# Four-layer graph network: layer 0's norm and first aggregate of the next batch placed in the tail of the present one

## The reference

```python
# layer 0: aggregate, two linear maps with an RMS norm and silu between
neighbor_sum = jnp.einsum('bnm,bmd->bnd', adjacency, x); agg = epsilon * x + neighbor_sum
h = silu(_rmsnorm(agg @ W1 + b1, rms_weight)); out = h @ W2 + b2          # 256 -> 1024 -> 256
# layer 1: one linear map, sigmoid(s1_i + s2_j) * adj, rows divided by their sums
# layer 2: masked attention, 8 heads of 32, edge bias W_e[h] * adj, softmax over 512
# layer 3: D^-1/2 adj D^-1/2 (x @ weight) + bias
```

## Time and profile before

| | before |
|---|---|
| median of 3 runs (lowest to highest) | 3917.56 us (3916.5 to 3918.57) |
| the profiled execution, its own time | 3917.78 us |
| its span | 3916.0 us |
| PE busy | 3609.4 us, 92% of the span |
| DVE / ACT / POOL busy | 67% / 58% / 21% |
| mean granted TensorE clock | 0.994 |
| mean busy share of 16 DMA engines, q1 | 26.2% |

### The profile page before, as it was taken

How to read it: one execution, slowest core, us unless ns; L and a number is a source line. 1 busy time by engine, 2 the same in 40 slices (tenths; PEclk the granted TensorE clock), 3 DMA queues, 4 the chain that set the end, 5 groups by cost and what they waited for, 6 DMA issues and landing times.

```text
span 3916.0 us, 67010 instructions
## 1 busy us (share of the span) xinstructions
PE 3609.4 (92%) x19375; PEld 2448.1 (63%) x19596; DVE 2623.3 (67%) x6436; ACT 2273.2 (58%) x5029; POOL 824.0 (21%) x1611
## 2 busy tenths in 40 slices
PE   5899999999999999999999999999999999999997
PEld 3566666666666666666666666666666666666664
DVE  4566766667666666666667666676666676666674
ACT  2555665555665556655556655556655566655564
POOL 1122111222112222212221122221122221122210
PEclk9899999999999999999999999999999999999999
DMA  2222222322222322223222223222233222232212
GB/s 77 60 78 75 64 67 64 86 65 75 65 67 73 85 66 65 75 54 86 72 78 59 70 65 86 65 70 70 57 83 81 70 65 75 54 86 68 78 48 65
DMA packets 166929, 274.99 MB, mean 70 GB/s; under 512 B 23906, under 2 KB 59874, under 8 KB 166756
## 3 DMA queue, kind: packets, MB, share of 16 engines
q1 hardware_dynamic: 166756, 273.45, 26.2%
HBM read 122.37 MB, written 16.78 MB: 36 GB/s over the span
## 4 chain that ended last, share of the span: by engine, by line
PE 45%; issue 26%; DVE 14%; POOL 9%; ACT 5%; POOLq 1%; SPq 0%; DVEq 0%; DMA 0%; ACTq 0%; another core or an unknown queue 0%
PE turn L1186 9%; PE front L999 6%; PE front L1000 5%; PE score L1176 5%; PE front L1001 5%; POOL small L366 4%; PE score L1177 4%; PE value L1201 3%; PE front L1052 3%; DVE pT L788 2%; ACT hf L485 2%; PE front L1041 2%; DVE hid L780 2%; DVE small L840 2%; POOL x_out L430 2%
## 5 line engine op out<-in xcount | busy, mean ns | idle before, releaser
L574 ACT ACTIVATE prob<-prob,small 128x512 f32<-128x512 f32 x1024 | 736.2, 719 | 443.6 <-DVE small L863 442.0
L863 DVE CUSTOM_DVE_ANT_0 prob<-score,adj_sb,drv 128x512 f32<-128x512 f32 x1024 | 762.4, 747 | 252.0 <-PE score L1177 133.7
L1186 PE MATMUL turn<-ident,prob 128*128 128x128 f32 x4096 | 616.1, 275 | 14.8 <-ACT pT L583 8.9
L1186 PEld LDWEIGHTS turn<-ident,prob 128*128 128x128 f32 x4096 | 483.5, 141 | 135.5 <-issue 45.7
L583 ACT ACTIVATE pT<-turn 128x512 f32<-128x512 f32 x768 | 446.6, 584 | 143.4 <-PE turn L1186 143.4
L1176 PE MATMUL score<-qk_stack 128*128 128x512 f32 x1024 | 486.9, 479 | 20.7 <-DVE small L863 19.1
L999 PE MATMUL front<-w_hi,s_hi 128*128 128x256 f32 x1024 | 353.7, 345 | 28.1 <-DVE x_in L767 28.1
L655 DVE TENSOR_TENSOR s_lo<-front,s_hi 128x512 fp32r<-128x512 f32 x320 | 219.1, 685 | 154.1 <-ACT s_hi L471 152.3
L1177 PE MATMUL score<-unlinked,neg_mask 128*128 128x512 bf16 x803 | 313.8, 391 | 0.0
L388 POOL TENSOR_TENSOR small<-small 128x1 f32<-128x1 f32 x128 | 24.7, 193 | 1265.7 <-ACT aside L518 1265.7
L1000 PE MATMUL front<-w_lo,s_hi 128*128 128x256 f32 x1024 | 288.6, 282 | 0.0
(11 more groups left out here) (158 smaller groups left out, 7547.7 us busy)
## 6 DMA issues: line engine op xcount, KB each, us to landing
qk_stack<-qk SPq DMA_DIRECT2D x1024, 128.0 KB, 2.4
adjT_f<-in_adjT SPq DMA_DIRECT2D x32, 1024.0 KB, 5.2
adj_sb<-in_adj SPq DMA_DIRECT2D x32, 1024.0 KB, 7.9
prob<-in_adjT SPq DMA_DIRECT2D x32, 1024.0 KB, 5.3
x_in<-in_x SPq DMA_DIRECT2D x32, 512.0 KB, 3.5
out<-x_out SPq DMA_DIRECT2D x32, 512.0 KB, 2.9
pT<-in_W SPq DMA_DIRECT2D x2, 1024.0 KB
rmsw_b<-in_rmsw SPq DMA_DIRECT2D x1, 512.0 KB
```

The costliest lines, as they stand in the source:

```text
L574: act.activation(prob[:, i % 8, :], prob[:, i % 8, :], ACT.Exp, bias=nmax[:, h, n:n + 1], scale=-1.0, accum_out=prsum[:, h, n:n + 1]).then ...
L863: dve.tensor_tensor_reduce(out=prob[:, i % 8, :], in0=SB_[i % 2][:, :], in1=adj_sb[:, n, :], scale=neg_w[:, h:h + 1], scalar=3e38, op0=ALU ...
L1186: last = pe.transpose(TB[k % 2][:, tile(n)], prob[:, (4 * h + n) % 8, tile(j)], ident[:, :])
```

## The change

Batch nx = tf+1 enters a phase. Its layer-0 norm and aggregate are done in the tail of the phase (t, tf), instead of at the opening of the next one.

- PE: `aggregate` is cut in two. Its first half stands after `aggregate3(t, 1)`, then come `turn(tf)` (which had opened the next phase), `project3(t)`, and the second half. The next phase opens with the Q and K projections, then `hidden` of row tile 0, a half of the values, the other `hidden`, the other half. Those two `hidden` products and their squares are no longer in the grid.
- DVE: `stats0(nx)` ahead of layer 1's two low parts, `diagonal(nx)` ahead of `update1`, the low parts of the aggregate and the copy of `turn` around `update3`.
- ACT: the norm of nx between `attended1` and `gathered`; POOL: its scale ahead of `add_b3`, and `add_b2` at the end of the phase.
- SP: x of the following batch is loaded at the start of a phase, ahead of the stacks, into a buffer of its own.
- Buffers: `x_new` is added (x as loaded; `add_b2` writes x_in from it). The normed x of layer 0 (`h0`) lies in `hid`. `x_out` now lies over `qk`, so ACT's first write of `qk` in a phase waits for the store of the batch before. Layer 3's high and low parts lie over `vals` and `unlinked` and not in T_hi and T_lo; `inv_x` lies over `hb`.

```diff
+        x_new = sb("x_new", [P, NT, D])
+        h0 = hid[:, :].rearrange("p (n d) -> p n d", n=NT)
-        x_out = sb("x_out", [P, NT, D])
+        x_out = sb("x_out", [P, NT, D], over="qk")
+        a3_hi = sb("a3_hi", [P, DT, N], F32R, over="vals")
+        a3_lo = sb("a3_lo", [P, DT, N], F32R, over="unlinked")
...
+            def phases(t, tf, nx):          # SP
+                if nx is not None:
+                    sp.wait_ge(b2_added, at(tf, 1, 1))
+                    sp.wait_ge(f_norm["ready"], at(tf, 8, 4))
+                    load_x(nx)
                 if t is not None:
+                    for h in range(H):
+                        stack(t, h)
...
             def add_b2(tf):                 # POOL
-                pool.wait_ge(f_norm["ready"], at(tf, 8, 4))
+                pool.wait_ge(x_loaded, at(tf, 16, 16))
+                if later(tf):
+                    pool.wait_ge(x1_ready, at(tf, 4, 0))
...
                     layernorm(t, 1, b_norm, norm_tiles(50), dinv)
+                if nx is not None:
+                    layernorm(nx, 0, f_norm, norm_tiles(0))
+                if t is not None:
                     add_b3(t)
...
             def qk_high(t, g, i):           # ACT
                 act.wait_ge(qk_ps, at(t, 4, 2 * g + i + 1))
+                if g == 0 and i == 0 and later(t):
+                    act.wait_ge(out_stored, t * 16)
...
                     attended1(tf, 1)
+                if nx is not None:
+                    norm0(nx)
                 if b:
                     gathered(t, 0)
                     gathered(t, 1)
                 if f:
                     layernorm(tf, 0, b_norm, norm_tiles(50), x2, hf)
+                if nx is not None:
+                    aggregated(nx, 0)
+                if f:
+                    turned(tf)
+                if nx is not None:
+                    aggregated(nx, 1)
...
                     update2(t)              # DVE
                     means(t, 1, b_norm, norm_tiles(50))
+                if nx is not None:
+                    stats0(nx)
                 if f:
                     attended1(tf, 0)
                     attended1(tf, 1)
                     factors1(tf)
+                if nx is not None:
+                    diagonal(nx)
                 if f:
                     update1(tf)
                     means(tf, 0, b_norm, norm_tiles(50))
                 if b:
                     gathered(t, 0)
                     gathered(t, 1)
+                if nx is not None:
+                    aggregated(nx, 0)
+                if f:
+                    turned(tf)
+                if b:
                     update3(t)
+                if nx is not None:
+                    aggregated(nx, 1)
+                    restore_diagonal(nx)
...
                 if b:                       # PE
-                    turn(t)
                     project_qk(t, 0, 0)
                     project_qk(t, 0, 1)
+                if f:
+                    hidden(tf, 0, 0)
+                if b:
                     project_v(t, 0)
                 if f:
-                    aggregate(tf)
+                    hidden(tf, 0, 1)
                 if b:
                     project_v(t, 1)
...
                     aggregate3(t, 1)
+                if nx is not None:
+                    aggregate(nx, 0)
+                if f:
+                    turn(tf)
+                if b:
                     project3(t)
+                if nx is not None:
+                    aggregate(nx, 1)
```

More of the change, by code:

```diff
@@ L111, in gnn_kernel @@
         msg = region[:, 5120:6144].rearrange("p (n d) -> p n d", n=NT)
-        inv_x = sb("inv_x", [P, NT, HG, HD], over="x_out")
+        inv_x = sb("inv_x", [P, NT, HG, HD], over="hb")
         small = sb("small", [P, 236])
@@ L431, in add_b3, with phases @@
                 ins.then_inc(b3_added, 1)
[L433 to L436, removed]
+            def phases(t, tf, nx):
                 if t is not None:
@@ L457, in phases @@
                     layernorm(tf, 0, b_norm, norm_tiles(50))
-            phases(None, 0)
-            phases(0, 1)
-            with pool.Fori(1, B - 1) as t:
-                phases(t, t + 1)
-            phases(B - 1, None)
+                if nx is not None:
+                    add_b2(nx)
+            layernorm(0, 0, f_norm, norm_tiles(0))
+            add_b2(0)
+            phases(None, 0, 1)
+            phases(0, 1, 2)
+            with pool.Fori(1, B - 2) as t:
+                phases(t, t + 1, t + 2)
+            phases(B - 2, B - 1, None)
+            phases(B - 1, None, None)
         @block.scalar
@@ L912, in update3, with phases @@
                                              in1=x_out[:, n, :], op0=ALU.mult, op1=ALU.add).then_inc(out_ready, 1)
-            def opening(t, tf):
-                b, f = t is not None, tf is not None
-                if b:
-                    turned(t)
-                if f:
-                    stats0(tf)
-                    diagonal(tf)
-            def rest(t, tf):
+            def phases(t, tf, nx):
                 b, f = t is not None, tf is not None
@@ L1017, in _, with aggregate @@
             pe.wait_ge(setup_dve, SETUP_DVE)
-            def aggregate(tf):
-                pe.wait_ge(f_norm["ready"], at(tf, 8, 4))
-                pe.wait_ge(diag_eps, at(tf, 1, 1))
-                if later(tf):
-                    pe.wait_ge(x1_ready, at(tf, 4, 0))
-                for d in range(DT):
-                    for m in range(NT):
-                        last = pe.matmul(FB[d][:, :], hf[:, m, tile(d)], adjT_f[:, m, :], start=(m == 0), stop=(m == NT - 1))
-                    last.then_inc(agg_ps, 1)
+            def aggregate(tf, d):
+                if d == 0:
+                    pe.wait_ge(f_norm["ready"], at(tf, 8, 4))
+                    pe.wait_ge(diag_eps, at(tf, 1, 1))
+                    if later(tf):
+                        pe.wait_ge(msg_ready, at(tf, 4, 0))
+                for m in range(NT):
+                    last = pe.matmul(FB[d][:, :], h0[:, m, tile(d)], adjT_f[:, m, :], start=(m == 0), stop=(m == NT - 1))
+                last.then_inc(agg_ps, 1)
             def hidden(tf, n, c):
@@ L1232, in step @@
                 def step(n, k, start, stop):
-                    return product(proj3_bank(n), (T_hi[:, k, tile(n)], T_lo[:, k, tile(n)]),
+                    return product(proj3_bank(n), (a3_hi[:, k, tile(n)], a3_lo[:, k, tile(n)]),
                                    (w3_hi[:, k, :], w3_lo[:, k, :]), start, stop)
```

128 lines of the change are left out of this document (63 added, 65 removed).

## The result

| | before | changed |
|---|---|---|
| median (lowest to highest) | 3917.7 us (3916.5 to 3918.57) | 3794.1 us (3793.83 to 3796.3) |
| span of the profiled execution | 3916.0 us | 3792.0 us |
| PE busy | 3609.4 us, 92% | 3595.9 us, 95% |
| ratio, 95% interval | | 0.9686 (0.9669 to 0.9703) |

The change saves 123.6 us, 3.2%. 3813 was forecast, a saving of 104.8, so the direction and the range held and the size was 15% short.

The account below looks back on a forecast made before the run. PE's matmul stream was taken as the bound, with only its idle time to win: 3917.8 - 102 (30 full boundaries) - 5 (first boundary) + 2 (last) = 3812.8, so 3813 us, range 3790 to 3850.

Parts of the forecast that it names:

- PE's stream is the bound and its idle time at the boundary is the prize: Between phases: PE's matmuls bound the kernel; of some 7.2 us idle a period, 4.6 stand at the boundary.
- 3.4 us a boundary: Each of 30 boundaries between full phases: idle time falls from 4.62 to 1.2 us, 102 us in all.
- The 1.2 us that I left idle: Idle left at a boundary: 0.15 at the turn, 0.05 in project3, 1.0 over scores 2, 3 and 4.
- Which part gives what: At the boundary: aggregate's move removes waits of 0.88, 0.97 and 0.93 us; hidden's earlier place removes the silu's 1.29.
- The four tail queues take the work at no cost: Phase tail: DVE, ACT, POOL and SP fit the added work into gaps, the diagonal with 0.5 us to spare.
- First boundary, 5 us: After the front-half-only phase: half the aggregate fills 3.55 us, 0.97 goes, the grid's start gains about 0.8.
- Last boundary, 2 us lost: Last boundary, no batch to aggregate: the turn waits for hf, and ACT for the store; 2 us slower.
- The two covers: Full phases: x_out's store has 1.6 us of cover before Q's high part, 1.1 more until K's; stacks have 1.3.
- Rival C: Opening: store or stacks land late and stop it; decides at 6.9 us, gain gone at 10.3; chance 0.06.
- Rival B: Phase tail: POOL's add holds DVE, the update starts 1.5 us late, saving 1.9 a boundary, 3858 us; chance 0.13.
- Rival E: Boundary: score waits smaller than counted and other waits shrink too, saving 4.2 to 4.6 us, middle 3783; chance 0.07.

Follow-up runs that it names:

- run 1: The changed kernel with row tile 0's two hidden products and squares back in the grid, values directly after the Q and K projections: 3863.9 us, ratio 0.9867.
- Run 3: The changed kernel with three extra 128x512 copies on DVE between the diagonal and layer 1's update: 3829.2 us, ratio 0.9773.
- run 7: The kernel before with 7 extra 128x512 matmuls on constants in the first phase's tail, where PE idles: 3918.4 us, ratio 1.0000.
- run with 512 KB: The changed kernel with an extra 512 KB DMA (rows of x) issued by SP just ahead of the store of x_out: 3848.1 us, ratio 0.9824.
- run with 1 MB: The changed kernel with an extra 1 MB DMA (adjacency rows) issued by SP just ahead of the store of x_out: 3927.5 us, ratio 1.0023.

## Why the prediction was right, point by point

- *PE's stream is the bound and its idle time at the boundary is the prize*: right. 4.60 us of idle became 0.95, the rest of the period stayed.
- *3.4 us a boundary*: the mechanism was right, the term too small. A boundary saves 3.92. The 1.2 us that I left idle were 0.95, of them 0.90 in two score waits of 0.55 and 0.35, not three of 0.5, 0.1 and 0.4, and none in project3. The turn did lose to hf, 0.4 us and not 0.1 to 0.2, but inside PE's busy time. That busy time still fell by 0.2 where I held it fixed, with the same matmuls: a wait also costs the overlap of the last matmul with the next (the first half of the values takes 1.89 us up to the wait for hf in the kernel before, and 1.54 up to the next group in the changed one), and there are fewer waits. The rest, some 0.1 us, lies outside the boundary. 30 times 0.5 is 16 of the 19 us that the forecast was short; the first and the last boundary add 3.3 and take 1.3.
- *Which part gives what*: this was wrong. I gave 2.6 us to the aggregate and the turn and 0.8 to `hidden`'s place; run 1 says 1.7 and 2.2, in that order of the steps. The sum came out near all the same, as it counts the waits and not what fills each. An operation that is moved away from a wait also uncovers what it had covered.
- *The four tail queues take the work at no cost*: right, with 0.30 us to spare at the update instead of 0.5. Run 3 shows that beyond it the cost is full.
- *First boundary, 5 us*: from the end of the linear products of the first phase (120.20; 119.11 in the changed kernel) to the end of layer 3's aggregate in the next, 124.2 us became 115.9. That is 8.3. Of it 1.9 is the granted clock (run 7), which I had not priced: 6.17 us idle had dropped it, 2.25 and 0.40 do not.
- *Last boundary, 2 us lost*: from the end of layer 3's aggregate in the last full phase to the end of the span, 100.3 us became 103.6. 3.3 lost; the places were as told. The mean granted clock of the stretch is 0.93 where it was 0.95, so part of the loss may be the clock's; how much, no run shows.
- *The two covers*: for the store on ACT right within 0.2 us, as it lands 1.4 us before ACT writes Q's high part in the full phase. For the stacks wrong: in the loop the last DMA that score 0 needs lands 0.3 us ahead of it, and score 0 never follows such a landing by less than 0.1 where it waits for it, so 0.2 are to spare and not 1.3. Two terms were off. PE's fill is 6.35 us and not 7.1, since each group begins under the end of the one before. And the path takes 6.05 and not 5.8, since DVE is not there when Q's high part is ready but comes back from the jump of its loop 1.2 us later, which leaves the stacks 0.3 later; in the kernel before, the stacks had 4.2 to spare (not "over 5") and hid this. For the whole path from store to score I had 4.0 us (1.6, 1.1 and 1.3); it is 3.1, read outside the loop.
- *Rival C's price*: it was to decide at a landing of 6.9 us, with the gain gone at 10.3. With 1 MB ahead the store lands at 6.9 and the gain is gone there already. About half of a wait there is DVE's late return, and a period grows by twice the wait, by the clock; I had neither.
- *Rival B*: it did not come, since `add_b3` ended before the diagonal. Rival E asked for 4.2 to 4.6 us a boundary and 3.92 were measured; its half about smaller score waits was right.

## What to carry to other kernels

Price PE's idle time at each wait, then ask of each group of matmuls that is moved not only which wait it fills at its new place but which one it had filled at the old; a run that moves one group alone settles it. Follow a late event to the last engine that depends on it before calling it covered, and look at what else the same load delays: here the store had 3.1 us of cover, and PE waited for an engine on its way back to the start of a loop. Don't put an instruction that others wait for first behind such a jump without 3 us to spare. And order the opening so that what a DMA must fetch is produced first: the version that does so, and splits the values, saved 22 us beyond the change itself.

## What the runs showed of the hardware

A wait of PE costs more than its length where the clock falls behind it. 6.17 us of idle were followed by a granted clock of 0.50 and 0.73 in the next 12 us, 2.27 us by 0.67 and 0.76, and a period grew by twice the wait; waits of about 1 us left it at 1.00 in most periods and lowered it in a few, while one of 1.75 us (run with 512 KB, the interval from 2574.07) and one of 2.71 (run with 1 MB, the interval from 359.14) left it at 1.00. In run 3 waits of 1.30 and 2.25 us close together in the first tail were followed by 0.72 (124 to 130); the 2.25 alone, in the changed kernel, by 1.00. So the length of a wait alone doesn't say whether the clock falls. The Trainium skill, "TensorE: Matmul & The Clock Gate", section "HAM oscillation — how this bites in real kernels", describes waits for DMA that throttle TensorE again in each turn of a loop; the run with 1 MB ahead of the store is such a case, in 28 of its 29 intervals with a wait of over 1 us.

DVE pays for each jump back in its loop: 2.7 to 3.0 us pass before its next instruction, while ACT and POOL go on after some 0.2 us. In each of the 28 returns of the kernel before, of the changed one and of both runs with a load ahead of the store, one transfer of 8 KB on the queue that the profile calls "instruction" starts between the jump and the return, 1.8 to 2.0 us ahead of the return. With 512 KB and 1 MB more in SP's queue the return takes 4.2 to 5.0 and 5.3 to 6.0 us. That it waits for this transfer is read from the times; no run takes the transfer away.

Large DMAs in one queue overlap and each makes the next ones later. A store of 512 KB that is issued 0.56 us behind a load of 1 MB and 1.16 us ahead of a load of 512 KB takes 6.9 us instead of 3.1, the load behind it 7.6 instead of 3.7, and the one ahead 6.0, where other loads of 1 MB take 5.3. They land in the order of issue, 1.4 and 2.0 us apart (period from 1791.32).
